# Projection stage of a strided-attention kernel: natural key order on TensorE, no counts copy, and two steps started at other points

## The reference, cut to what matters

```python
xn = _layernorm(x)                       # mean and variance per row of 256
q, k, v = xn @ q_w, xn @ k_w, xn @ v_w   # 16 heads of 16
allowed = (j % 4 == 0) | (abs(i - j) <= 8)
attn = softmax(where(allowed, q k^T, -inf)) @ v
x_dq = clip(xn / input_scale, -448, 448).astype(float8_e4m3fn) * input_scale
x = x + (attn @ o_w + o_b) + (x_dq @ (weight_fp8 * weight_scale).T + bias)
```

## Time and profile before

| | |
|---|---|
| median of 3 runs | 1312.47 us (1310.71 to 1314.17) |
| the profiled execution's own time | 1312.86 us |
| its span, first to last instruction | 1311.0 us |
| TensorE matmul busy over the span | 1241.9 us (95%) |
| VectorE busy | 1019.3 us (78%) |
| ScalarE busy | 847.5 us (65%) |
| GpSimd busy | 248.4 us (19%) |

### The profile page before, as it was taken

How to read it: one execution, slowest core, us unless ns; L and a number is a source line. 1 busy time by engine, 2 the same in 40 slices (tenths; PEclk the granted TensorE clock), 3 DMA queues, 4 the chain that set the end, 5 groups by cost and what they waited for, 6 DMA issues and landing times.

```text
span 1311.0 us, 28302 instructions
## 1 busy us (share of the span) xinstructions
PE 1241.9 (95%) x9536; PEld 604.9 (46%) x9536; DVE 1019.3 (78%) x1863; ACT 847.5 (65%) x1540; POOL 248.4 (19%) x380
## 2 busy tenths in 40 slices
PE   5999999789999999899989998998999899999896
PEld 3667767424443344344434443443344344444385
DVE  5899998598888788688878886887888688888032
ACT  3445445237877677687767776776777677777700
POOL 2233233101111121111111211122121112121200
PEclk9999999869999999899999998999999899999998
DMA  7677779943545343535444453535254544442257
GB/s 166 201 218 229 227 222 183 278 76 84 120 117 112 97 114 106 121 91 123 107 105 108 117 119 89 121 103 116 90 121 112 105 108 112 109 119 85 88 202 282
DMA packets 220000, 177.10 MB, mean 135 GB/s; under 512 B 50384, under 2 KB 192848, under 8 KB 219792
## 3 DMA queue, kind: packets, MB, share of 16 engines
q1 hardware_dynamic: 213328, 168.05, 49.2%
q10 hardware_dynamic: 6528, 7.08, 1.6%
HBM read 105.98 MB, written 68.29 MB: 133 GB/s over the span
## 4 chain that ended last, share of the span: by engine, by line
PE 66%; SPq 5%; DMA 4%; issue 2%; DVE 1%; ACT 1%; ACTq 0%; DVEq 0%
PE ps_attend L981 18%; PE ps_attend L937 16%; PE ps_attend L962 16%; PE ps_attend L943 4%; PE ps_attend L988 4%; PE ps_attend L966 4%; PE ps_attend L1082 3%; SPq L83 2%; DMA k_op<-k_parts_dram 2%; DMA sums<-sums_dram 1%; SPq L76 1%; DVE peak_far L900 1%; DMA q_op<-attn_dram 1%; PE ps_attend L934 1%; SPq L77 1%
## 5 line engine op out<-in xcount | busy, mean ns | idle before, releaser
L900 DVE TENSOR_REDUCE peak_far<-ps_attend 128x1 f32<-128x512 f32 x1024 | 652.5, 683 | 140.6 <-PE ps_attend L962 140.5
L845 ACT ACTIVATE probs<-ps_attend 128x512 f32<-128x512 f32 x1024 | 562.9, 597 | 153.3 <-PE ps_attend L937 152.8
L962 PE MATMUL ps_attend<-k_op,q_op 96*128 96x512 bf16 x1024 | 361.6, 393 | 35.2 <-issue 23.1
L937 PE MATMUL ps_attend<-q_op,k_op 128*128 128x512 bf16 x1024 | 341.8, 385 | 2.7 <-ACT probs L850 1.5
L981 PE MATMUL ps_attend<-probs,v_op 128*32 128x512 f32 x2048 | 277.3, 614 | 0.7 <-ACT probs L845 0.7
L937 PEld LDWEIGHTS ps_attend<-q_op,k_op 128*128 128x128 bf16 x1024 | 100.0, 98 | 191.2 <-ACT probs L845 109.1
L850 ACT ACTIVATE probs<-ps_attend 108x512 f32<-108x512 f32 x256 | 153.5, 600 | 44.5 <-PE ps_attend L943 44.5
L903 DVE TENSOR_REDUCE peak_near<-ps_attend 128x4 f32<-128x432 f32 x256 | 153.9, 601 | 21.4 <-PE ps_attend L966 21.2
L726 POOL CAST negmax<-peak 128x16 bf16<-128x16 f32 x64 | 12.6, 196 | 753.0 <-DVE peak L911 753.0
L962 PEld LDWEIGHTS ps_attend<-k_op,q_op 96*128 96x128 bf16 x1024 | 93.0, 98 | 98.5 <-issue 45.6
L943 PEld LDWEIGHTS ps_attend<-q_op,k_op 128*108 128x108 bf16 x1024 | 89.2, 128 | 86.7 <-ACT probs L845 54.9
(11 more groups left out here) (66 smaller groups left out, 944.4 us busy)
## 6 DMA issues: line engine op xcount, KB each, us to landing
q_op<-q_parts_dram SPq DMA_DIRECT2D x384, 64.0 KB, 2.7
k_op<-k_parts_dram SPq DMA_DIRECT2D x96, 192.0 KB, 4.3
v_dram<-v_sb SPq DMA_DIRECT2D x64, 256.0 KB, 3.1
share_rows<-shares_dram SPq DMA_DIRECT2D x64, 256.0 KB
attn_dram<-out_rows SPq DMA_DIRECT2D x64, 256.0 KB, 3.9
v_op<-v_dram SPq DMA_DIRECT2D x48, 288.0 KB
q_parts_dram<-qk_parts SPq DMA_DIRECT2D x48, 256.0 KB, 3.8
k_parts_dram<-qk_parts SPq DMA_DIRECT2D x48, 192.0 KB, 2.5
```

Of the source, the lines that this page charges most:

```text
L845: ins = nc.scalar.activation(probs[:, r, h], ps_s[st.bank(kind)], ACT.Exp)
L900: ins = nc.vector.tensor_reduce(peak_far[:, h, tile:tile + 1], bank, AX_X, ALU.max)
L937: ins = nc.tensor.matmul(bank, k[:, h * SK + r * P:h * SK + (r + 1) * P], q[:, h], start=True, stop=True)
L962: ins = nc.tensor.matmul(bank, q[0:KR, h, cols], k[0:KR, h * SK:h * SK + NS], start=True, stop=True)
```

## The change

Five edits, all in `part_project`:
- TensorE multiplies the keys in their natural order: 4 matmuls of 512 columns in place of 4 of 128 and 4 of 384.
- The sorting by stride moves behind it: ScalarE's copy of the high part of the keys and VectorE's key subtraction become two instructions each, one for every fourth key and one for the others, read with a stride and written to where they were written before.
- VectorE's copy to `counts`, which nobody reads, is gone, and the wait on `stat` in front of it stands, in the loop, ahead of the query subtraction.
- GpSimd's L262 no longer waits for `lo_ready` (VectorE's low part of the keys of the chunk before). It still waits for `power_ready` and `f_ready`.
- VectorE's key subtraction stands ahead of `deviation`, no longer behind it.

```diff
--- before.py
+++ after.py
@@ -106,7 +106,6 @@
         scales = sb("scales", [P, 4])
         unity = sb("unity", [P, 3])
         stats = sb("stats", [P, TT, 6])
-        counts = sb("counts", [P, TT])
         mv = sb("mv", [P, TT, 2])
         var = sb("var", [P, TT])
         dev = sb("dev", [P, TT])
@@ -174,6 +173,16 @@
 
             return CPB // 2 * j + n // 2
 
+        def in_order(keys):
+
+            keys = keys.rearrange("p i (g r) -> p i g r", r=STRIDE)
+            return keys[:, :, :, 0], keys[:, :, :, 1:]
+
+        def by_stride(keys):
+
+            ns = CH // STRIDE
+            return keys[:, :, 0:ns], keys[:, :, ns:].rearrange("p i (g r) -> p i g r", r=STRIDE - 1)
+
         @block.sync
         def _(sp):
             sp.dma_start(x_in[:, 0], x_rows[0]).then_inc(x_loaded[0], 16)
@@ -258,7 +267,6 @@
                 pool.wait_ge(power_ready, c + 1)
                 if not (isinstance(c, int) and c < 1):
                     pool.wait_ge(f_ready, c)
-                    pool.wait_ge(lo_ready, 2 * c)
                 nc.gpsimd.tensor_tensor(quant[:], quant[:], power[:], ALU.add).then_inc(sum_ready, 1)
                 pool.wait_ge(sum_ready, c + 1)
                 pool.wait_ge(hi_ready, 2 * c + 1)
@@ -310,7 +318,9 @@
                 deviation(j, n, 2)
                 if main:
                     act.wait_ge(k_ready, c + 1)
-                    nc.scalar.activation(qk_parts[:, k, 1, 0], ps_k, ACT.Copy).then_inc(hi_ready, 1)
+                    for to, src in zip(by_stride(qk_parts[:, k, 1, 0]), in_order(ps_k)):
+                        last = nc.scalar.activation(to, src, ACT.Copy)
+                    last.then_inc(hi_ready, 1)
                     act.wait_ge(rest_ready, 2 * c + 2)
                     nc.scalar.activation(qk_parts[:, k, 1, 1], rest[:, 1], ACT.Copy).then_inc(mid_ready, 1)
                     act.wait_ge(v_ready, c + 1)
@@ -355,8 +365,8 @@
                 if isinstance(c, int) and c > B * CPB - 1:
                     return
                 done = 7 * c
-                dve.wait_ge(stat, done + 1)
-                nc.vector.tensor_copy(counts[:], stats[:, :, 0])
+                if isinstance(c, int):
+                    dve.wait_ge(stat, done + 1)
                 for t in range(TT):
                     last = nc.vector.bn_aggr(mv[:, t], stats[:, t])
                 last.then_inc(stat, 1)
@@ -398,7 +408,12 @@
                 dve.wait_ge(hi_ready, 2 * c + w + 1)
                 if not (isinstance(c, int) and c < 1):
                     dve.wait_ge(lo_ready, 2 * c + w - 1)
-                nc.vector.tensor_tensor(rest[:, w], src, qk_parts[:, k, w, 0], ALU.subtract).then_inc(rest_ready, 1)
+                if w == 0:
+                    last = nc.vector.tensor_tensor(rest[:, w], src, qk_parts[:, k, w, 0], ALU.subtract)
+                else:
+                    for to, of, hi in zip(by_stride(rest[:, w]), in_order(src), by_stride(qk_parts[:, k, w, 0])):
+                        last = nc.vector.tensor_tensor(to, of, hi, ALU.subtract)
+                last.then_inc(rest_ready, 1)
 
             def fp8_power(j, n):
                 c, k = CPB * j + n, n % 2
@@ -425,15 +440,18 @@
                 if main and not (isinstance(c, int) and c < 1):
                     add_linear(c - 1)
                 row_stats(j, n + 2)
+                if not isinstance(c, int):
+                    dve.wait_ge(stat, 7 * (c + 2) + 1)
                 if main:
                     cut(c, k, 0)
                 variance(j, n + 2)
                 fp8_power(j, n + 1)
                 if isinstance(c, int) and c == -1:
                     prepare_linear()
+                if main:
+                    cut(c, k, 1)
                 deviation(j, n + 2)
                 if main:
-                    cut(c, k, 1)
                     low_part(c, k, 0)
                 normalise(j, n + 2)
                 if main:
@@ -492,13 +510,10 @@
 
                     if not (isinstance(c, int) and c < 1):
                         pe.wait_ge(rest_ready, 2 * c)
-                    grouped = xnT[:, k].rearrange("p i (g r) -> p i g r", r=STRIDE)
-                    ns = CH // STRIDE
                     for m in range(KC):
-                        for cols, keys in ((slice(0, ns), grouped[:, :, :, 0]), (slice(ns, CH), grouped[:, :, :, 1:])):
-                            for i in range(KC):
-                                last = nc.tensor.matmul(ps_k[:, m, cols], wk[:, i, m * P:(m + 1) * P], keys[:, i],
-                                                        start=(i == 0), stop=(i == KC - 1))
+                        for i in range(KC):
+                            last = nc.tensor.matmul(ps_k[:, m], wk[:, i, m * P:(m + 1) * P], xnT[:, k, i],
+                                                    start=(i == 0), stop=(i == KC - 1))
                     last.then_inc(k_ready, 1)
 
                     if not (isinstance(c, int) and c < 1):
```

## The result

The changed kernel takes 1351.74 us (median of 4 runs, 1348.58 to 1353.96), the kernel before 1311.72 us (1310.71 to 1314.17). The ratio is 1.0295, interval [1.0268, 1.0323]: slower, as forecast, but above the forecast's range of 1309 to 1341. The profiled execution took 1348.58 us with a span of 1346.8, against 1312.86 and 1311.0: its span is 35.8 us longer, where the prediction had 23.

A forecast was written before the change was run, and what follows sets the result against it. TensorE bounds the kernel, a VectorE-ScalarE loop next; twelve periods of 13.85 + 2.2 us plus 1.3 in the first chunk give +24.7, less 1.6 covered: 23 us more, 1336 us. Range 1309 to 1341, the forecast's own 1331 to 1341.

The forecast's parts named there:

- the two loops: Projection period: TensorE's own sum of 13.97 us, and a loop through VectorE and ScalarE of 13.8 us, next to limit.
- Keys in natural order: TensorE's key matmuls: 3.46 us in place of 4.42, saving 0.96 a period, of which about 0.15 reaches the time.
- The copy dropped: VectorE's copy to counts: removal saves nothing, since the wait for ScalarE's scaled copy grows by what the copy took.
- Two instructions for one: Split key subtraction on VectorE adds 0.05 us a period; ScalarE's extra key copy fits in its slack.
- The low end: Cost of VectorE's split, strided key subtraction: 0.05 us a period taken, from bounds of 0.05 to 0.6.
- The rival of dear strides: Strided reads cost VectorE 0.3 us a period, with no stall: 1314 us, at the full bound 1317; chance 0.07.
- The key subtraction moved: Subtraction ahead of deviation stays in VectorE's unbroken run, so the loop is as long: nothing gained, nothing lost.
- The first addition unheld: GpSimd's addition falls on VectorE's normalise and stalls it through the shared port, 2.2 us a period; chance 0.60.
- The rival that VectorE keeps the port: GpSimd's addition waits until VectorE's run of instructions ends, so no stall: 1310.5 us; chance 0.28.
- Chunk 0: First chunk of the projection: the addition meets the small deviation operations, about 1.3 us more.
- SyncE's queue covers 1.6 us of the last stall: End of projection: the last keys' store waits behind value stores anyway, hiding 1.6 us before the attention part's first loads.
- Nothing in that part changes.: The attention part behind the projection was taken to keep its length, adding nothing to the growth.

The follow-up runs named there:

- e4: Changed kernel with GpSimd's first addition made to wait for VectorE's normalise, in place of the removed wait for the low parts; 1323.43 us, ratio 1.008.
- e5: e4 with 48 small unused matmuls added to TensorE's code in the projection part, 24 in the first chunk, 24 at its end; 1309.53 us, ratio 0.9994.
- e1: Changed kernel with the removed wait of GpSimd's first addition for VectorE's low part of the keys restored; 1323.83 us, ratio 1.0082.
- e3: Kernel before with only the natural key order and its split key copy and subtraction; 1324.53 us, ratio 1.0093.
- e8: Changed kernel with GpSimd's wait for f_ready moved behind its first addition, which then starts as soon as fp8_power is done; 1337.11 us, ratio 1.0175.
- e2: Kernel before with only the wait of GpSimd's first addition for VectorE's low part of the keys removed; 1330.8 us, ratio 1.0143.
- e7: Changed kernel with 48 small unused matmuls added to TensorE's code ahead of the attention loop; 1340.86 us, ratio 1.022.
- e12: Kernel before with 32 small unused matmuls added to TensorE's code ahead of the attention loop; 1307.11 us, ratio 0.9964.
- e9: e4 with 16 small unused matmuls added to TensorE's code ahead of the attention loop; 1302.86 us, ratio 0.9923.
- e6: Kernel before with 16 small unused matmuls added to TensorE's code ahead of the attention loop; 1321.48 us, ratio 1.0061.

## Why the prediction was right or wrong

- **The bound, and the two loops.** TensorE and the loop of 13.8 us through VectorE and ScalarE were read rightly: with GpSimd out of the way (e4, e5) the period is 13.8. A third loop was missed. With the hold in place GpSimd's two additions stand in it (e1, e3: 13.97 us). Its sign was in a row that the prediction read: ScalarE's L308 waits 0.20 us for L265.
- **Keys in natural order.** Right in the matmuls, which take 3.43 us a chunk (126.63 to 130.06), and in that almost nothing reaches the time: of the 0.96 us saved nothing is seen in e3's periods. That e3 is held by the third loop, and not by VectorE's of 13.85, was not foreseen.
- **The copy dropped: nothing.** Right: L359 is gone, and VectorE's wait for the scaled copy is 1.67 us where it was 0.70. No run removed it alone.
- **Two instructions for one.** Right: the two L415 start 1.20 us before what follows (132.47 to 133.67) in place of 1.14 for L401, 0.06 more. The low end held: reading every fourth element costs nothing that shows. The rival of dear strides is refuted.
- **The key subtraction moved: nothing.** It stays in VectorE's run, and L415 isn't stopped by GpSimd (e8).
- **The first addition unheld.** Right in place and kind. The stall is 2.03 us a period (taken as 2.2, bounds 2.0 to 2.45), and the twelve periods average 192.29 / 12 = 16.02 us, against 16.05. That the average fits so well is in part luck: 13.8 + 2.03 gives 15.83, as in the period shown, and the rest is the four periods with the slow clock. The prediction had foreseen the clock, but as a later `f_ready` and a smaller stall; in the slow period from 140.14 on the stall is 2.1 us and the period 0.5 longer. The rival that VectorE keeps the port is refuted by the changed kernel and by e2, where the addition comes inside the four instructions of `normalise` and gets its turn ahead of the rest of them. The price of the stall by itself is e7 against e5, which differ in the hold alone: 1340.86 - 1309.53 = 31 us.
- **Chunk 0.** A term of the sum was mis-sized: taken as 1.3 us, it was 3.7. The first addition stops L388 for 2.1 us, and the second, L273, then falls on chunk 0's `normalise` (38.88, 3.40 us), 2.0 more; the changed kernel had come there 0.5 us earlier than the kernel before. This is one execution's price. In e7, with the same code there, the first addition falls on `normalise` and nothing else is stopped, 2.0 us (the rows are in the last section).
- **SyncE's queue covers 1.6 us of the last stall.** It does at the first load (24.8 us later, where 3.7 + 23.1 would give 26.8). But the pads' clearing, with which the attention part begins, is 27.3 us later: it doesn't follow that load. From L351 to it there is a thirteenth period with a stall (16.41 us in place of 13.94), and two last ones that are 2.0 us shorter together, 0.5 us in all. The step should have gone on to the last chunk.
- **"Nothing in that part changes."** This is the step that failed, and its 8.5 us in the profile is the largest miss. The code of the part is the same, but its place in TensorE's code is not: at each turn of its loop TensorE waits twice for code in place of once, 28.5 us in place of 22.5, and then runs longer at the lower clock. By medians the changed kernel gains 1351.74 - 1340.86 = 11 us from 48 unused matmuls (e7), and the held one 1323.43 - 1309.53 = 14 us (e4, e5). With the place of before, the forecast holds: e7's 1340.86 us is at the upper end of its 1331 to 1341.

Against the sum of 1336 the profiled execution is 12.6 us longer: 2.4 from chunk 0, -0.3 from the twelve periods, 2.1 from the cover that wasn't one, 8.5 from the attention part, to within rounding. The median lies 3.2 us over that execution, which was the fastest of four.

**What stays open.** No profile shows which instruction a packet ends on, so that the place of the loop in it is known only modulo 64 matmuls, at four values. Why one wait a turn takes 2.9 us at one place (e12) and 3.8 at another (before) isn't shown, nor why TensorE keeps its full clock behind three of e9's six turns. Dropping the copy and moving the key subtraction were not tried alone.

## What to carry to other kernels

A wait that looks superfluous may be what keeps GpSimd off VectorE's fast instructions: before it goes, look up which VectorE instruction the freed one will meet. Here the best hold let it start just behind the `tensor_scalar` instructions, beside a long one with two SBUF inputs that was already running, so that GpSimd waited 0.9 us and that addition stopped nothing of VectorE (e4). The stall that this saves is 31 us of 1341 (e5 against e7). An edit that changes the number of instructions ahead of a hardware loop moves the loop, and each comparison must be made part by part of the span, or with the count filled up to the same place. When the bounding engine gets less work, look for the loops that come next with every engine in them, GpSimd too.

## What the runs showed that was not expected

- The shared port goes in turns. An addition that arrives during a VectorE instruction with two SBUF inputs waits for that one only (0.9 us in e4, 0.4 in e2), and stops the next VectorE instruction that it can stop. In e4 and e2 none follows at once. In chunk 0 of e7 one does: L270 comes 0.35 us into L434, takes 3.07 us, 0.7 over its 2.36, and `normalise` behind it takes 3.40 (rows below the list). The Trainium skill says that whoever issues first gets the pair for the whole instruction (SBUF — State Buffer, Who interferes with whom); both halves are seen here.
- Being short doesn't protect from the stall: an instruction on 4 elements with two SBUF inputs waited 1.0 us (e8), one on 4 elements with a constant, L388, 2.1 (chunk 0 of the changed kernel). Both ended with the addition.
- Code alone, with nothing else changed, moved the kernel before between 0.9964 and 1.0061 of itself (e12, e6).

The rows of e7, chunk 0:

```profile
35.35 1.22 DVE L434 TENSOR_TENSOR qk_parts<-rest,qk_parts 128x1024 bf16<-128x1024 f32 x1
35.70 3.07 POOL L270 TENSOR_TENSOR quant<-quant,power 128x1024 f32<-128x1024 f32 x1 [5.96 <-PE ps_project L543]
...
36.49 3.40 DVE L401 TENSOR_SCALAR xn<-base,mv,rstd 128x256 f32<-128x256 f32 x4
```
